# The first feed-forward sequence brought forward into the last tiles of the local attention

## The reference, cut to what matters

```python
def _layer(x, wqkv, qs, ksc, wo, lg, lb, w1, b1, w2, b2):
    h = shift_token(x)
    q, k, v = jnp.split(h @ wqkv, 3, axis=-1)            # 8 heads of 64
    q = l2norm(q) * qs;  k = l2norm(k) * ksc
    q, k = rotary_xpos(q, k)
    x = x + local_attention(q, k, v) @ wo                # window 64, one block looked back
    h = shift_token(x)
    h = (h - mu) / jnp.sqrt(var + 1e-05) * lg + lb       # layer norm over the 128 channels
    a, g = jnp.split(h @ w1 + b1, 2, axis=-1)            # 2 x 341 hidden channels
    return x + (a * gelu(g, exact)) @ w2 + b2
...
x = x + 0.5 * _L0_ffn_ref(_layernorm(x), ...)            # site 0: two layers
x = x + _L0_attn_ref(_layernorm(x), ...)
x = x + 0.5 * _L0_ffn_ref(_layernorm(x), ...)            # site 1: two layers
x = x + 0.5 * _L1_ffn_ref(...);  x = x + _L1_attn_ref(...);  x = x + 0.5 * _L1_ffn_ref(...)
```

## Time and profile before

| | |
|---|---|
| median of 3 runs (lowest, highest) | 1364.35 us (1364.29, 1367.82) |
| the profiled execution: its own time, its span | 1367.0 us, 1365.2 us |
| PE busy | 1193.8 us (87%) |
| PEld (weight loads, beside PE) | 883.0 us (65%) |
| DVE busy | 964.7 us (71%) |
| ACT busy | 847.8 us (62%) |
| POOL busy | 823.5 us (60%) |
| mean granted TensorE clock | 0.959 of full speed |

### The profile page before, as it was taken

One profiled execution on the slowest core, in us unless ns is written; L12 is line 12 of the kernel. 1 busy time (PEld: TensorE's weight loads), 2 busy tenths in 40 slices (PEclk: granted clock), 3 DMA queues, 4 the chain that ended last, 5 costly groups with the idle time before them and its releaser, 6 DMA issues. The chain is left out here.

```text
span 1365.2 us, 36481 instructions
## 1 busy us (share of the span) xinstructions
PE 1193.8 (87%) x12629; PEld 883.0 (65%) x12630; DVE 964.7 (71%) x2520; ACT 847.8 (62%) x2470; POOL 823.5 (60%) x872
## 2 busy tenths in 40 slices
PE   4899898999888888969998999989879867889994
PEld 2567685766755555536776767768479854648984
DVE  5899768998766666769996699968844346674334
ACT  2899858998544444459997689984435534234552
POOL 5899638998454343159994589954167741117772
PEclk9999999999989999999999999999879998878998
DMA  6001100011000000000111001113157740017764
GB/s 211 20 21 25 35 10 19 21 25 25 21 11 3 3 3 3 3 1 17 25 25 28 16 9 24 31 27 79 31 169 228 206 141 0 1 31 212 225 205 133
DMA packets 71571, 79.26 MB, mean 58 GB/s; under 512 B 26791, under 2 KB 52070, under 8 KB 71270
## 3 DMA queue, kind: packets, MB, share of 16 engines
q1 hardware_dynamic: 65765, 65.49, 16.9%
q0 software_dynamic: 5632, 11.55, 3.2%
HBM read 55.52 MB, written 8.91 MB: 47 GB/s over the span
## 5 line engine op out<-in xcount | busy, mean ns | idle before, releaser
L853 POOL TENSOR_TENSOR rnp<-ss,mhalf 128x16 f32<-128x16 f32 x64 | 186.3, 2912 | 21.1 <-DVE ss L703 20.1
L2085 DVE SCALAR_TENSOR_TENSOR act_b<-bank,vec,gl 128x128 f32<-128x128 f32 x264 | 76.7, 345 | 136.7 <-ACT gl L1908 106.7
L1824 PE MATMUL bank<-arena 128*128 128x128 f32 x1056 | 138.7, 283 | 1.7 <-issue 0.8
L1824 PEld LDWEIGHTS bank<-arena 128*128 128x128 f32 x1056 | 129.2, 197 | 6.0 <-issue 3.7
L2129 POOL DMA_INDIRECT arena<-u_rows,inv_u x88 | 86.6, 984 | 74.6 <-DVE inv_u L2056 44.0
L785 ACT ACTIVATE pA<-bank,nb,rn 128x128 f32<-128x128 f32 x256 | 113.3, 464 | 12.6 <-DVE nb L714 12.6
L785 ACT ACTIVATE pB<-bank,nb,rn 128x128 f32<-128x128 f32 x256 | 113.3, 462 | 10.5 <-DVE nb L714 10.2
L848 POOL TENSOR_TENSOR arena<-arena 128x512 f32<-128x512 f32 x64 | 104.7, 1636 | 14.5 <-DVE arena L678 14.3
L1908 ACT ACTIVATE gl<-bank,vec 128x128 f32<-128x128 f32 x264 | 77.9, 366 | 54.0 <-PE bank L1824 39.2
L1599 DVE TENSOR_REDUCE act_b<-bank 128x2 f32<-128x512 f32 x128 | 79.5, 685 | 39.3 <-PE bank L1482 39.3
L2135 POOL DMA_INDIRECT y_rows<-stg,inv_u x88 | 86.5, 983 | 33.8 <-issue 20.4
(11 more groups left out here) (332 smaller groups left out, 3253.9 us busy)
## 6 DMA issues: line engine op xcount, KB each, us to landing
arena<-in_L_ffn_We SPq DMA_DIRECT2D x88, 384.0 KB
arena<-arena SPq DMA_DIRECT2D x64, 128.0 KB, 2.3
arena<-in_L_ffn_We SPq DMA_DIRECT2D x3, 768.0 KB, 7.3
arena<-U SPq DMA_DIRECT2D x32, 64.0 KB
u_rows<-U SPq DMA_DIRECT2D x2, 1024.0 KB, 5.2
U<-y_rows SPq DMA_DIRECT2D x8, 256.0 KB, 4.5
uT<-y_rows SPq DMA_DIRECT2D x8, 256.0 KB, 4.8
arena<-U SPq DMA_DIRECT2D x32, 63.5 KB
```

The source lines that it names most:

```text
L853: pool.tensor_tensor(rnp[:, :], ss[:, 1, :], mhalf[:, :], ALU.pow).then_inc(s.rn_self, 1)
L1824: m = pe.matmul(bank[q % 2][:, j * P:(j + 1) * P], we1[q][:, half * HR + j * P:half * HR + (j + 1) * P], xT[:, q, :], start=True, stop=True)
```

## The change

The first sequence of the feed-forward is started while the attention still works on its last tiles.

- `stats(0)` on DVE goes ahead of `step(12)`, `normed(0)` ahead of `step(14)`; `stats(1)` stays where it was.
- `h_power(0)` on POOL goes ahead of `step(13)`, that is ahead of `k_scaled(13)`.
- `turned(0)` on PE goes into `step(14)`, behind `q_turn(15)`, and writes bank 0 in place of bank 3.
- `h_out(0)` on ACT goes into `step(14)`, behind `v_out(14)` and ahead of `pt_out(14, 0)`.
- `up(0)` is split. Its chunk 0 goes to bank 0 and is issued between `step(14)` and `step(15)` on PE; chunk 1 goes to bank 1 and is issued inside `step(16)`, between `turn(15, 0)` and `turn(15, 1)`; chunk 2 stays in bank 6, behind `pv(15)`. The waits follow the banks: chunk 0 for `hT2` and the last `rope` of Q, chunk 1 for the last `rope` of K, chunk 2 for the last `pt_out`.
- `gelu(0)` and `act(0, c)` read the banks where the chunks now are; their place in the lists does not change. No instruction is added or taken away, and none changes its size.

The diff, cut to its core (layer 1 and the sites repeat the edits of layer 0):

```diff
-            def step(q):
+            def step(q, turned=None, up=None):
                 def has(d):
                     return 0 <= q + d < NT
 
@@ -647,12 +647,16 @@
                     q_proj(q + 2)
                 if has(-1):
                     turn(q - 1, 0)
+                if up:
+                    up(0, 1)
                 if has(0):
                     sims(q)
                 if has(-1):
                     turn(q - 1, 1)
                 if has(1):
                     q_turn(q + 1)
+                if turned:
+                    turned(0)
                 if has(-2):
                     out_proj(q - 2)
...
+                if h_out:
+                    h_out(0)
                 if has(0):
                     pt_out(q, 0)
...
-        MT, MG, MY, MX = B[3], (B[4], B[5], B[6]), B[7], B[2]
+        MT, MY, MX = B[3], B[7], B[2]
+
+        def up_bank(b, c):
+            return B[c] if b == 0 and c < 2 else B[4 + c]
+
+        def turn_bank(b):
+            return MT if b else B[0]
...
-                else:
+                if b == 0:
+                    pe.wait_ge(s.rq_ab, (pb + 1) * NT)
+                elif b == 1:
                     pe.wait_ge(s.kT_ready, (pb + 1) * NT)
                 for t in range(2):
-                    m = pe.transpose(MT[:, t * P:(t + 1) * P], hn[:, t * P:(t + 1) * P], ident[:, :])
+                    m = pe.transpose(turn_bank(b)[:, t * P:(t + 1) * P], hn[:, t * P:(t + 1) * P], ident[:, :])
                 m.then_inc(s.hnT_ps, 1)
 
+            def up_chunk(b, c):
+                h0, n = HCH[c]
+                pe.wait_ge(s.hT2_ready, hb + b + 1)
+                if b == 0 and c == 0:
+                    pe.wait_ge(s.ld_w, 16 * (pb + 1))
+                if b == 0 and c < 2:
+                    pe.wait_ge((s.rq_ab, s.rk_ab)[c], (pb + 1) * NT)
+                elif b == 0:
+                    pe.wait_ge(s.pT_ready, 2 * (pb + 1) * NT)
+                elif b == 1 and c < 2:
+                    pe.wait_ge(s.exp_done, 2 * (pb + 1) * NT)
+                else:
+                    pe.wait_ge(s.act_ready, 3 * (hb + b - 1) + c + 1)
+                for g in range(2):
+                    m = pe.matmul(up_bank(b, c)[0:n, g * SEQ:(g + 1) * SEQ], w1[:, g * HID + h0:g * HID + h0 + n],
+                                  hT2[:, :], start=True, stop=True)
+                m.then_inc(s.up_ps, 1)
+
             def up(b):
-                pe.wait_ge(s.hT2_ready, hb + b + 1)
-                for c, (h0, n) in enumerate(HCH):
-                    if b:
-                        pe.wait_ge(s.act_ready, 3 * (hb + b - 1) + c + 1)
-                    elif c == 0:
-                        pe.wait_ge(s.exp_done, 2 * (pb + 1) * NT)
-                        pe.wait_ge(s.ld_w, 16 * (pb + 1))
-                    elif c == 2:
-                        pe.wait_ge(s.pT_ready, 2 * (pb + 1) * NT)
-                    for g in range(2):
-                        m = pe.matmul(MG[c][0:n, g * SEQ:(g + 1) * SEQ], w1[:, g * HID + h0:g * HID + h0 + n], hT2[:, :],
-                                      start=True, stop=True)
-                    m.then_inc(s.up_ps, 1)
+                for c in range(len(HCH)):
+                    up_chunk(b, c)
...
+        STATS_AT = NT - 4
...
-            for q in range(1, NT):
+            for q in range(1, NT - 2):
                 lo0.step(q)
-            ff0(-1)
-            lo0.step(NT)
-            ff0(0)
+            lo0.step(NT - 2, turned=ff0.turned)
+            ff0.up_chunk(0, 0)
+            lo0.step(NT - 1)
+            lo0.step(NT, up=ff0.up_chunk)
+            ff0.up_chunk(0, 2)
+            ff0.step(0)
             lo0.step(NT + 1)
             for j in range(1, 5):
-                ff0(j)
+                ff0.step(j)
...
             for q in range(1, NT - 1):
+                if q == STATS_AT:
+                    ff0.stats(0)
+                if q == NT - 2:
+                    ff0.normed(0)
                 lo0.step(q)
                 if q == ALPHA_AT and not site:
                     dve.wait_ge(s.ld_late, 16 * N_LATE)
                     dve.scalar_tensor_tensor(alpha_w[:, 0, :], alpha[:, :], -1.0, alpha[:, :], ALU.mult, ALU.min)\
                         .then_inc(s.alpha_ready, 1)
-            ff0(-2)
             lo0.step(NT - 1)
-            ff0(-1)
+            ff0.stats(1)
             lo0.step(NT)
             lo0.step(NT + 1)
-            ff0(0)
+            ff0.step(0)
...
-                lo0.step(q)
+                lo0.step(q, h_out=ff0.h_out if q == NT - 2 else None)
                 if q == ALPHA_AT + 3 and not site:
                     act.wait_ge(s.alpha_ready, 1)
                     act.activation(alpha_w[:, 1, :], alpha_w[:, 0, :], ACT.Exp).then_inc(s.alpha_ready, 1)
             lo0.step(NT)
-            ff0(-1)
             act.preload_act_table(ACT.Gelu)
             lo0.step(NT + 1)
...
+                if q == STATS_AT + 1:
+                    ff0.h_power(0)
                 lo0.step(q)
```

More of the change, by code:

```diff
@@ L796, in v_out, with step @@
                 act.activation(vv[c][:, t, :], BV[:, :], ACT.Copy).then_inc(s.v_ready, 1)
-            def step(q):
+            def step(q, h_out=None):
                 def has(d):
@@ L883, in act_of @@
             return act_b[0:n, c, (b % 2) * SEQ:(b % 2 + 1) * SEQ]
+        FfPe = namedtuple("FfPe", "step turned up_chunk")
+        FfDve = namedtuple("FfDve", "step stats normed")
+        FfAct = namedtuple("FfAct", "step h_out")
+        FfPool = namedtuple("FfPool", "step h_power")
         def ff_pe(pe, l, pb):
@@ L956, in step @@
                     logits(j - 4)
-            return step
+            return FfPe(step, turned, up_chunk)
         def ff_dve(dve, l, pb, coef):
@@ L1019, in step @@
             def step(j):
[L1020 removed]
+                if 0 < j + 1 < NBATCH:
                     normed(j + 1)
@@ L1034, in step @@
                     x_normed(j - 2)
-            return step
+            return FfDve(step, stats, normed)
         def ff_act(act, l, pb):
@@ L1044, in gelu @@
                     r = l * 6 + V_B1 + 3 + c
-                    act.activation(gl_of(b, c, n), MG[c][0:n, SEQ:2 * SEQ], ACT.Gelu, bias=vec[0:n, r:r + 1])\
+                    act.activation(gl_of(b, c, n), up_bank(b, c)[0:n, SEQ:2 * SEQ], ACT.Gelu, bias=vec[0:n, r:r + 1])\
                         .then_inc(s.gelu_done, 1)
@@ L1049, in h_out @@
                 act.wait_ge(s.hnT_ps, hb + b + 1)
-                act.activation(hT2[:, :], MT[:, 0:SEQ], ACT.Identity, bias=vec[:, l + V_LB:l + V_LB + 1],
+                act.activation(hT2[:, :], turn_bank(b)[:, 0:SEQ], ACT.Identity, bias=vec[:, l + V_LB:l + V_LB + 1],
                                scale=vec[:, l + V_LG:l + V_LG + 1]).then_inc(s.hT2_ready, 1)
@@ L1063, in step @@
                     x_out(j - 2 - l)
-            return step
+            return FfAct(step, h_out)
         def ff_pool(pool, l, pb):
@@ L1097, in step @@
                     x_power(j - 1)
-            return step
+            return FfPool(step, h_power)
+        STATS_AT = NT - 4
         def site_pe(pe, site, ph):
@@ L1228, in site_dve @@
             lo1.rope(0, 1)
-            ff0(6)
+            ff0.step(6)
             lo1.rope(0, 0)
             lo1.squares(0)
-            ff0(7)
+            ff0.step(7)
             lo1.rope(1, 1)
-            ff0(8)
+            ff0.step(8)
             for q in range(NT - 1):
+                if q == STATS_AT:
+                    ff1.stats(0)
+                if q == NT - 2:
+                    ff1.normed(0)
                 lo1.step(q)
-            ff1(-2)
             lo1.step(NT - 1)
-            ff1(-1)
+            ff1.stats(1)
             lo1.step(NT)
             lo1.step(NT + 1)
-            ff1(0)
+            ff1.step(0)
             lo1.step(NT + 2)
             for j in range(1, NBATCH + 2):
-                ff1(j)
+                ff1.step(j)
             if not site:
@@ L1303, in site_act @@
             lo1.qk_out(0, 0)
-            ff0(8)
+            ff0.step(8)
             lo1.square(1, 0)
-            ff0(9)
+            ff0.step(9)
             lo1.qk_out(0, 1)
@@ L1309, in site_act @@
             for q in range(NT):
-                lo1.step(q)
+                lo1.step(q, h_out=ff1.h_out if q == NT - 2 else None)
             lo1.step(NT)
-            ff1(-1)
             act.preload_act_table(ACT.Gelu)
@@ L1343, in site_pool @@
             for j in range(-2, 8):
-                ff0(j)
+                ff0.step(j)
             for q in range(-1, NT):
+                if q == STATS_AT + 1:
+                    ff1.h_power(0)
                 lo1.step(q)
             for j in range(-2, NBATCH + 1):
-                ff1(j)
+                ff1.step(j)
                 if not site and 0 <= j < NBATCH:
```

45 lines of the change are left out of this document (24 added, 21 removed).

## The result

The changed kernel takes 1373.23 us (median of 7, 1372.02 to 1374.77); the kernel before took 1367.29 beside it (median of 7, 1362.5 to 1368.74). The ratio on record is 1.0054 (the two medians alone give 1.0043), 95% interval 1.0041 to 1.0068: slower, by well under 2%. Measured four times more it was 1.0083, 1.0071, 1.0063 and 1.0096. The profiled execution has a span of 1369.9 us and an own time of 1372.46.

A forecast was written before the change was run, and what follows sets the result against it. It took each seam to be bound by the chain of waits from the last scores to pv(15). Per seam +2.22 + 0.5 - 1.57 = +1.15 us, four +4.6, gave 1368.8 us; range 1362.5 to 1372.0, its own 1366.7 to 1371.2.

The forecast's parts named there:

- The stall, +2.22 a seam: On PE, chunk 0 waits for h_out(0) ahead of turn(14, 0) and the last scores, making them 2.22 us late.
- The gain behind `pv(15)`, -1.57: With chunks 0 and 1 already in their banks, pv(15) to up(1) falls from 3.87 to 2.30 us.
- The early norms, +0.5: Early stats(0), normed(0) and h_power(0) delay DVE and POOL in the steps before the scores; 0.5 us a seam.
- DVE's delay of 0.46: On DVE, stats(0) delays by 0.27 us and normed(0) by 0.19, beyond the 0.41 us idle in a step.
- POOL's of 0.46: On POOL, h_power(0) takes about 1.0 us; two steps' idle time take 0.56, leaving power(15) 0.46 us late.
- the rival in which it is shut out: DVE's early norm blocked by POOL through shared ports, up to 0.7 us more a seam, 1371.7; chance 0.09 with low clock.
- The sum, +1.15 a seam, +4.6: Stall plus norms minus gain: +1.15 us a seam, +4.6 for four; own time near 1371.6 from the profiled execution.
- the forecast's own range: Total time of 1366.7 to 1371.2 us, from seams costing 0.6 to 1.7 us, half way to the bounds.
- against the median of 1364.35 it gives 1368.9: Step taking the profiled execution as 2.65 us above the median, so 1371.6 became 1368.9, stated as 1368.8.
- Against it: 2.29 us of idle time at 218 to 220 left four transposes at the 0.66 us: Argument that about 2 us of PE idle time would not lower its clock, as transposes kept 0.66 us after 2.29 idle.
- that rival: PE standing still about 2 us behind k_turn(15) lowers its clock; no size given, chance 0.09 together with the slow norm.

The follow-up runs named there:

- Experiment 1: Changed kernel with chunk 0 of up(0) issued in step(15) behind turn(14, 1), so behind the last scores; ratio 0.9975 to the kernel before.
- experiment 3: Kernel before with one wait added on PE ahead of step(15), for v_out(14), and no work added; ratio 1.0028.
- experiment 5: Kernel before with only stats(0) and h_power(0) moved early, 1.0027; also Experiment 1 with h_power(0) behind q_sum(14), 0.9982.
- program shifted: Changed kernel with 24 small matmuls and waits ahead of TensorE's second group of instructions, to move later program packets; ratio 1.0124.
- second site alone: Change's order only in the second site's two feed-forwards, the first site in old order with the new banks; ratio 1.0035.
- the filled: Changed kernel with eight identity transposes into bank 1 while TensorE waits for h_out(0) ahead of chunk 0; ratio 1.0068.
- banks alone: Changed kernel's new banks and waits, but every instruction of sequence 0 in its old place; run twice, ratios 1.0019 and 1.0008.

## Why the prediction was wrong

*The stall, +2.22 a seam: right.* 2.27 in the first three seams and 2.33 in the fourth, and it reaches `pv(15)` whole: from the scores to `v_out(15)` 6.70 us for 6.73, from there to `pv(15)` 3.67 for 3.66. Experiment 1 takes it away and the loss turns into a gain; experiment 3 has a stall of 0.9 us alone.

*The gain behind `pv(15)`, -1.57: right.* 1.59 by the rows at 354.59 and 356.87, 1.50 to 1.59 to `down(0)`.

*The early norms, +0.5: right in size, half right in cause.* 0.59 in seams 2 and 3, 0.88 in the first, 0.23 in the fourth. I set DVE's delay of 0.46 beside POOL's of 0.46. DVE's part for the norm was nothing: experiment 5 has the same 24.63 us without it. For `stats(0)` the same is argued only, from the idle 0.41 us and a product that took 1.00 in place of 1.47. POOL's part was 0.60: its idle 0.28 us was given up only once, where I had counted on twice (0.27 us is back ahead of the next power, at 334.18), and of the 0.7 us left its two additions in that step took back 0.18. The norm itself kept its 0.60 us, so the rival in which it is shut out did not come.

*The sum, +1.15 a seam, +4.6: right in mechanism and nearly in size for an undisturbed execution.* Four seams gave +5.1, and the own time of the profiled execution was 1372.46 where the sum made it 1371.6.

*From the sum to the range: wrong, in two steps.* The first, which puts the measured time outside the forecast's own range, is "against the median of 1364.35 it gives 1368.9". I took 2.65 us off because the profiled execution lay above the median of three runs. Later medians of the kernel before were 1367.29, 1367.23 and 1366.35: the profiled execution had been the typical one and the three runs the low ones. This step alone puts the range too low by 2.65 us: the forecast from the profiled execution is 1371.6, and 1373.23 was measured. The other 1.6 us have about the size of what its profile shows beyond the sum: 0.5 us in the seams, 0.9 in the stage behind the first site and 0.6 around the span. Its seams met neither the low clock nor a late copy. What follows shows in the later runs. The second is "Against it: 2.29 us of idle time at 218 to 220 left four transposes at the 0.66 us". That was one execution. Behind the same idle time in the start of the second layer the changed kernel's first profile shows

```profile
221.63 1.11 PE L567 MATMUL bank<-ident_sb,arena 128*128 128x128 f32 x4 [2.29 <-POOL arena L839]
```

at half the clock, where the earlier trace rows has 0.66. A fall of the clock at that place is in 12 of the 20 profiles, in two of three of the kernel before, and not in the one that I read. Idle time of 2.0 to 2.3 us of PE was followed by the low clock in some executions here and not in others. I gave that rival 0.09 together with the slow norm, and no price of its own; in place of it the runs show 1.6 to 1.7 us for a seam in which the clock falls within 1.1 us of the start of chunk 0 (2 of the 20 seams of the change's five profiles, 2 of 4 with the program shifted, none of 2 in the second site alone; none of 44 in kernels without this wait). The late copy stood in no part of the prediction; it has 2.6 to 3.0 us (3 of the 20).

*How the rest adds up.* The mean of the change's five profiles is 177.8 us of seams, +7.4. From the start of the stage behind the first site to its fourth block it takes 15.9, 18.5, 17.2, 15.4 and 18.2 us, where the kernel before needs 15.0: there too the clock stays low for longer, +2.0 in the mean. And between span and own time lie 2.4 to 2.6 us on the average of a group, where the kernel before has 1.83: +0.65. Together 10.0 us, 0.71 to 0.73%, and the mean of the five ratios is 1.0073. That holds in the mean only. The fourth profiled execution lies 5.8 us above its group's median of the kernel before where these parts make some 10, and the fifth 19.3 where they make some 14, so other stretches move by several us as well. The rows of the stage, second profile of the change, the same work at the low and at the full clock:

```profile
425.82 2.09 PE L1570 MATMUL bank<-arena 32*128 32x256 f32 x16
...
431.86 1.15 PE L1570 MATMUL bank<-arena 32*128 32x256 f32 x16
```

The clock was low there for 6.8 to 13.7 us in four of the change's five profiles (the fourth, where I expected it again, had 3.4) and in the filled and the shifted kernel, and for 3.4 in eleven of thirteen of the kernels with another order. The two others are the second profile of banks alone and the second site alone (6.8), so that the order in the seams makes it is not shown, nor why the clock rises late. What makes the 0.65 us around the span stays open as well; banks alone has it (2.3 and 2.4), the filled and the shifted kernel have not (1.83).

## What to carry to other kernels

Work moved into idle time of an engine must be ready when its turn comes. PE kept the order of its queue here: chunk 0 waited 2.00 us and handed its wait to the transposes and the scores behind it; ask of each moved piece what it waits for, and put it behind the instruction that the chain needs. Here four matmuls a few instructions later turned a loss of 0.5 to 1.0% into a gain of 0.25%.

A new wait on TensorE can have a second price, its clock, that a single profile may not show (4 of 26 seams with this wait of 2.00 us): look at several before idle time is called free. And add a sum made from a profiled execution to that execution's own time, not to the median of three runs.

## What the runs showed that I had not expected

- A packet that I take for TensorE's program can hold a critical copy. In five of five seams in which one began among the packets of the copy of 128 KB, `pv(15)` came 1.3 to 1.9 us late. No run moved the packet at will, so this rests on the times in five cases, with the copy's own late packets beside them.
- A 128x16 `tensor_scalar` on VectorE, 0.17 us by itself, was held for 1.06 us by a GpSimd addition. GpSimd's power, 2.91 us, did not hold the product at 325.94, which ran beside it in 0.73 us.

```profile
325.94 0.73 DVE L694 TENSOR_TENSOR pA<-pA,rden 128x512 f32<-128x512 f32 x1
```
